# Splitting the gate and value products of a fused feed-forward into three fp32r products

## The reference

```python
def attn_layer(x, Wqkv, qs, ksc, Wo):          # 16 heads of 64, windows of 32, keys of two windows
    q, k, v = jnp.split(x @ Wqkv, 3, -1)
    q, k = rotate(l2norm(q) * qs), rotate(l2norm(k) * ksc)
    return local_attention(q, k, v) @ Wo

def ffn_layer(x, g, bln, W1, b1, W2, b2):
    mu = x.mean(-1, keepdims=True)
    var = ((x - mu) ** 2).mean(-1, keepdims=True)
    xn = (x - mu) / jnp.sqrt(var + 1e-05) * g + bln
    hg = xn @ W1 + b1                           # W1 is 128 x 682
    a, gate = jnp.split(hg, 2, -1)              # 341 columns each
    return a * jax.nn.gelu(gate, approximate=False) @ W2 + b2

for i in range(6):
    x = attn_layer(shift_tokens(x), ...) + x
    x = ffn_layer(shift_tokens(x), ...) + x
```

## Time and profile before

| | us |
|---|---|
| median of 3 runs | 3869.65 (3862.52 to 3872.1) |
| the profiled execution | 3865.56 |
| its span in the profile | 3863.6 |
| layers, first to last projection | about 847 to 3777 |
| one step in the steady part | 61.3 |

### The profile page before, as it was taken

How to read it: one execution, slowest core, us unless ns; L and a number is a source line. 1 busy time by engine, 2 the same in 40 slices (tenths; PEclk the granted TensorE clock), 3 DMA queues, 4 the chain that set the end, 5 groups by cost and what they waited for, 6 DMA issues and landing times. The chain is left out here.

```text
span 3863.6 us, 161420 instructions
## 1 busy us (share of the span) xinstructions
PE 3682.6 (95%) x70608; PEld 2670.3 (69%) x70608; DVE 3257.1 (84%) x4767; ACT 2854.5 (74%) x5060; POOL 2384.6 (62%) x1968
## 2 busy tenths in 40 slices
PE   5899999958999999999999999999999999999997
PEld 3122222237888888888888888888888888888885
DVE  7899999947888888888888888888888888888884
ACT  2588888856777777777777777777777777777774
POOL 2100000047877777787777777777777777777783
PEclk7799999979999999999999999999999999999998
DMA  2110000014344444434444434444444344444442
GB/s 90 34 54 24 22 22 18 10 52 117 103 107 118 105 113 121 108 103 111 120 111 108 117 106 110 117 113 105 110 122 111 104 113 111 123 112 114 108 104 56
DMA packets 202559, 360.11 MB, mean 93 GB/s; under 512 B 35518, under 2 KB 74050, under 8 KB 201538
## 3 DMA queue, kind: packets, MB, share of 16 engines
q1 hardware_dynamic: 201794, 348.71, 33.8%
HBM read 236.68 MB, written 111.67 MB: 90 GB/s over the span
## 5 line engine op out<-in xcount | busy, mean ns | idle before, releaser
L1160 POOL TENSOR_TENSOR T<-T 128x1024 f32<-128x1024 f32 x384 | 908.5, 2378 | 26.7 <-DVE T L1639 25.8
L1178 POOL TENSOR_TENSOR T<-T,rn 128x1024 f32<-128x1024 f32 x384 | 731.1, 1904 | 27.1 <-POOL rn L1171 0.4
L745 ACT ACTIVATE E<-p_s 128x512 f32<-128x512 f32 x1024 | 556.1, 597 | 124.7 <-PE p_s L602 110.6
L1250 PE MATMUL PA<-Wqkv,XS 128*128 128x512 f32 x2304 | 634.2, 411 | 9.5 <-DVE XS L1600 8.7
L678 DVE TENSOR_REDUCE negmax<-p_max 128x1 f32<-128x1024 f32 x512 | 588.8, 1215 | 26.5 <-PE p_max L581 26.4
L1250 PEld LDWEIGHTS PA<-Wqkv,XS 128*128 128x128 f32 x2304 | 415.2, 194 | 80.1 <-DVE XS L1600 10.7
L1647 DVE TENSOR_REDUCE ss<-SQ 128x32 f32<-128x2048 f32 x192 | 436.9, 2275 | 0.0
L1326 PE MATMUL PB<-ET,VW 64*64 64x32 f32 x24576 | 400.7, 220 | 15.9 <-DVE T L1639 9.5
L1326 PEld LDWEIGHTS PB<-ET,VW 64*64 64x64 f32 x24576 | 378.8, 135 | 53.5 <-DVE T L1639 29.7
L1278 PE MATMUL PD<-ident,T 128*128 128x128 f32 x3072 | 409.3, 276 | 6.8 <-POOL T L1178 5.5
L1339 PEld LDWEIGHTS PD<-Wo,OT 128*128 128x128 f32 x3072 | 366.4, 192 | 61.7 <-issue 61.7
(11 more groups left out here) (168 smaller groups left out, 6762.4 us busy)
## 6 DMA issues: line engine op xcount, KB each, us to landing
VW<-v_rows SPq DMA_DIRECT2D x768, 256.0 KB, 4.5
v_rows<-Vs SPq DMA_DIRECT2D x192, 512.0 KB, 5.9
Wraw<-in_Wqkv SPq DMA_DIRECT2D x40, 192.0 KB, 5.2
QA<-parts_q SPq DMA_DIRECT2D x384, 16.0 KB
KA<-parts_k SPq DMA_DIRECT2D x192, 32.0 KB
parts_q<-parts SPq DMA_DIRECT2D x8, 384.0 KB, 2.6
parts_k<-parts SPq DMA_DIRECT2D x8, 384.0 KB, 2.7
Wo<-in_Wo SPq DMA_DIRECT2D x12, 256.0 KB, 4.6
```

Source lines behind the costliest of these rows:

```text
L745: act.activation(E[:, s % 4, c, :], p_s[:, (64 * g + i) % NS, :], ACT.Exp, scale=DH ** -0.5)\
L1160: pool.tensor_tensor(out=t_, in0=t_, in1=T2[:, i * HALF:(i + 1) * HALF], op=ALU.add).then_inc(ad.sem, 1)
L1178: pool.tensor_tensor(out=t_, in0=t_, in1=rn[:, p, i * LH:(i + 1) * LH].unsqueeze(2).broadcast_to([P, LH, LD]), op=ALU.mult).then_inc(no.se ...
L1250: mm = pe.matmul(pair[:, half, :], XS[:, b, i, 1:P + 1], Wqkv[:, l % 2, j, lo:lo + 512], start=(k == 0), stop=(k == 2))
```

## The change

The normalised tokens and `W1` are split into a high part (rounded to fp32r by ACT) and a low part (the rest, by POOL). Each of the six chunk products becomes three fp32r products. `W1` gets zeroed columns behind it, so that each chunk is 128 wide. `fnT` now shares memory with `fx`. Once in each layer ACT and POOL split the weights; once in each step they split the tokens. In PE's code the place of the instructions in the program is set to 98 where it was 100, for two of four slots.

```diff
+    FPAD = FF + NCH * P
+    W1 = m.sb("W1", [P, FPAD])
+    W1s = m.sb("W1s", [P, 2, FPAD], F32R)
+    fnT = fx[:, :, :].rearrange("p b c -> p (b c)")
+    fns = m.sb("fns", [P, 2, B * P], F32R)
 # SP, ahead of load_ff(u // NT)
+                sp.wait_ge(w1s.sem, w1s.at(u // NT - 1))
 # POOL
+        pool.memset(W1[:, 2 * FF:FPAD], 0.0).then_inc(s_one.sem, 1)
+        def ff_split(u):
+            pool.wait_ge(f3e.sem, f3e.at(u))
+            if u > 0:
+                pool.wait_ge(fv.sem, fv.at(u - 1))
+            pool.tensor_tensor(out=fns[:, 1, :], in0=fnT, in1=fns[:, 0, :].bitcast(F32), op=ALU.subtract)\
+                .then_inc(fnl.sem, 1)
+        def split_ff(l):
+            pool.wait_ge(w1s.sem, w1s.at(l, 1))
+            pool.tensor_tensor(out=W1s[:, 1, :], in0=W1[:, :], in1=W1s[:, 0, :].bitcast(F32), op=ALU.subtract)\
+                .then_inc(w1s.sem, 1)
             if is_tile(s - 1):
                 rotate(s - 1, 0)
+            if d == 1 and is_step(u - 2):
+                if (u - 2) % NT == 0:
+                    split_ff((u - 2) // NT)
+                ff_split(u - 2)
             if d == 2 and is_step(u + 1):
                 rotary_table(u + 1)
             if is_tile(s - 1):
                 rotate(s - 1, 1)
 # PE
-    BLOCK, FIRST_Q = 256, (105, 105, 100, 100)
+    BLOCK, FIRST_Q = 256, (105, 105, 98, 98)
+        def ff_product(i, lo):
+            for k, (x, y) in enumerate(((0, 0), (0, 1), (1, 0))):
+                mm = pe.matmul(PC[:, i % 2, :], W1s[:, y, lo:lo + P], fns[:, x, :], start=(k == 0), stop=(k == 2))
+            return mm
         def ff_gate(u, i):
             if i == 0:
                 pe.wait_ge(f3e.sem, f3e.at(u))
+                pe.wait_ge(fnl.sem, fnl.at(u))
+                pe.wait_ge(w1s.sem, w1s.at(u // NT))
-            pe.matmul(PC[0:c, i % 2, :], W1[:, FF + lo:FF + lo + c], fnT[:, :], start=True, stop=True)\
-                .then_inc(fg.sem, 1)
+            ff_product(i, FF + CH[i][0]).then_inc(fg.sem, 1)
         def ff_value(u, i):
-            pe.matmul(PC[0:c, i % 2, :], W1[:, lo:lo + c], fnT[:, :], start=True, stop=True).then_inc(fv.sem, 1)
+            ff_product(i, CH[i][0]).then_inc(fv.sem, 1)
 # ACT
         def ff_norm(u):
             act.wait_ge(s_wf.sem, s_wf.at(u // NT))
+            if u % NT == 0:
+                if u > 0:
+                    act.wait_ge(fv.sem, fv.at(u - 1))
+                act.activation(W1s[:, 0, :], W1[:, :], ACT.Copy).then_inc(w1s.sem, 1)
             act.wait_ge(f3.sem, f3.at(u))
             if u > 0:
+                act.wait_ge(fnl.sem, fnl.at(u - 1))
                 act.wait_ge(fv.sem, fv.at(u - 1))
-            act.activation(fnT[:, :], PC[:, 0, :], ACT.Identity, bias=ln[:, 1:2], scale=ln[:, 0:1])\
+            act.activation(fnT, PC[:, 0, :], ACT.Identity, bias=ln[:, 1:2], scale=ln[:, 0:1])\
                 .then_inc(f3e.sem, 1)
+            act.wait_ge(f3e.sem, f3e.at(u, 1))
+            act.activation(fns[:, 0, :], fnT, ACT.Copy).then_inc(f3e.sem, 1)
 # DVE, ff_tokens
-                dve.wait_ge(f3.sem, f3.at(u - 1))
+                dve.wait_ge(fnl.sem, fnl.at(u - 1))
```

More of the change, by code:

```diff
@@ L929, in layers @@
     KW = 2 * WIN
+    FPAD = FF + NCH * P
     Wraw = m.sb("Wraw", [P, share])
-    W1 = m.sb("W1", [P, 2 * FF])
+    W1 = m.sb("W1", [P, FPAD])
+    W1s = m.sb("W1s", [P, 2, FPAD], F32R)
     W2 = m.sb("W2", [P, NCH, D])
@@ L962, in layers @@
     frs = m.sb("frs", [P, B])
-    fnT = m.sb("fnT", [P, B * P])
+    fnT = fx[:, :, :].rearrange("p b c -> p (b c)")
+    fns = m.sb("fns", [P, 2, B * P], F32R)
     G = m.sb("G", [P, NCH, B * P])
@@ L1022, in layers @@
     f3 = m.count("l_f3")
-    f3e = m.count("l_f3e")
+    f3e = m.count("l_f3e", 2)
+    fnl = m.count("l_fnl")
+    w1s = m.count("l_w1s", 2)
     fg = m.count("l_fg", 3)
@@ L1032, in layers @@
     out = m.count("l_out", 16)
-    READY = 8
+    READY = 9
     def tile(n):
@@ L1056, in load_ff @@
             for dst, src in (
-                (W1[:, :], ins["W1"][l]),
+                (W1[:, 0:2 * FF], ins["W1"][l]),
                 (W2[:, 0:2, :], ins["W2"][l, 0:2 * P].rearrange("(a p) n -> p a n", p=P)),
@@ L1130, in on_pool @@
         pool.memset(zero[:, :], 0.0).then_inc(s_one.sem, 1)
+        pool.memset(W1[:, 2 * FF:FPAD], 0.0).then_inc(s_one.sem, 1)
         pool.memset(three[:, :], 1.5).then_inc(s_one.sem, 1)
-        pool.wait_ge(s_one.sem, 5)
+        pool.wait_ge(s_one.sem, 6)
         pool.memset(HH[lo:lo + 32, NCH - 1, :], 1.0).then_inc(s_one.sem, 1)
@@ L1366, in ff_norm @@
             mm.then_inc(f3.sem, 1)
-            fc_[0] = (f3e.sem, f3e.at(u))
+            fc_[0] = (f3e.sem, f3e.at(u, 1))
+        def ff_product(i, lo):
+            for k, (x, y) in enumerate(((0, 0), (0, 1), (1, 0))):
+                mm = pe.matmul(PC[:, i % 2, :], W1s[:, y, lo:lo + P], fns[:, x, :], start=(k == 0), stop=(k == 2))
+            return mm
         def ff_gate(u, i):
-            lo, c = CH[i]
             if i == 0:
                 pe.wait_ge(f3e.sem, f3e.at(u))
+                pe.wait_ge(fnl.sem, fnl.at(u))
+                pe.wait_ge(w1s.sem, w1s.at(u // NT))
             free(fc_[i % 2])
-            pe.matmul(PC[0:c, i % 2, :], W1[:, FF + lo:FF + lo + c], fnT[:, :], start=True, stop=True)\
-                .then_inc(fg.sem, 1)
+            ff_product(i, FF + CH[i][0]).then_inc(fg.sem, 1)
             fc_[i % 2] = (gd.sem, gd.at(u, i + 1))
         def ff_value(u, i):
-            lo, c = CH[i]
             free(fc_[i % 2])
-            pe.matmul(PC[0:c, i % 2, :], W1[:, lo:lo + c], fnT[:, :], start=True, stop=True).then_inc(fv.sem, 1)
+            ff_product(i, CH[i][0]).then_inc(fv.sem, 1)
             fc_[i % 2] = (hh.sem, hh.at(u, i + 1))
@@ L1697, in ff_down @@
                               op=ALU.add).then_inc(fxd.sem, 1)
-        dve.wait_ge(s_one.sem, 6)
+        dve.wait_ge(s_one.sem, 7)
         for j in range(2):
```

## The result

| | us, median (lowest to highest) | runs |
|---|---|---|
| before | 3870.88 (3862.52 to 3873.27) | 4 |
| after | 4125.57 (4123.97 to 4129.64) | 4 |

The ratio is 1.0664, with a 95% interval of 1.0645 to 1.0682: the change made the kernel 6.6% slower. The profiled execution took 4129.64 us, 264.1 more than the profiled one of before.

What follows compares the result with a forecast made beforehand. PE was taken as the bound, closely followed by POOL. 46 x (5.34 wait + 4.2 clock - 0.36 products) = 422, plus 7 + 1 for the layers, on 3865.56 gave 4295.6, so 4300 us; range 4095 to 4400.

Steps and rivals of the forecast that it cites:

- What bounds the kernel, and POOL's slack: PE is the bound; POOL can be kept about 2.93 us between its rotary additions and normalisations before PE waits.
- POOL's wait: POOL waits 7.0 us between the rotary additions for ACT's high part, moving PE's `attend` in slot 1 by 5.34 us.
- The prices: Durations of ACT's copy (0.63 us), POOL's token and weight subtractions (1.28, 1.8), and two gate chunks on PE (1.47).
- Value products: Three value chunks on PE in slots 2 and 3 save 0.375 us, counted as 0.36 us a step.
- Gate products: Gate chunks on PE in slots 1 and 2 save 0.375 us, given back as a wait for ACT's chain.
- The clock: PE's clock at 0.50 from slot 1's transposes of k in nearly every step, costing 4.2 us a step; bounds 0 to 6.5.
- the forecast's picture: Low clock in slot 1 over transposes of k, `attend` (1.6 us more), the projection of v and the first gate chunks.
- The rows at 885 and 3812: Earlier trace's ends of layers: after `attend` the low clock lasted 3.4 us of full work, around 885 5.6; middle 4.5.
- Code loading: Rival: PE's short stops in slot 1's scores no longer show, or new ones appear elsewhere; 20 us either way, no chance given.
- The clock holds: Rival: same wait on PE, but bursts of transposes keep the clock at 1.00; 4107 us, chance 0.17.
- the forecast's own case: POOL's wait and the clock's fall both cost time on PE's path; 4200 to 4400 us, chance 0.70.

Runs made afterwards that it cites:

- the placement behind both additions: The changed kernel with POOL's two subtractions moved behind the second rotary addition of the same loop; 4019.25 us, ratio 1.0400 against the kernel before.
- the filled gap: The changed kernel with 12 fp32r products put ahead of PE's wait for POOL in slot 1 of each step; 4104.1 us, ratio 1.0618 against the kernel before.

## Why the prediction was right in sign and mechanism, and wrong in size

- **What bounds the kernel, and POOL's slack: right.** 2.93 us of slack, read off and the earlier trace rows, is the point from which the wait counts, and the placement behind both additions confirms it with a second dose (3.13 us measured in its shortest slots, 3.05 by the sum).
- **POOL's wait: right.** Forecast 7.0 us, measured 7.02 in the step shown and 6.94 on the mean. PE's gap ahead of q was to be 3.4 and is 3.47. With the clock held, slot 1 has 19.56 to 19.60 in 34 of 39 steps, 5.5 over the 14.10 of before, where 5.34 was forecast.
- **The prices: right.** Copy 0.63 forecast and 0.632 measured, subtraction 1.28 and 1.290, the one on the weights 1.8 and 1.767. Two gate chunks were to take 1.47 and take 1.40.
- **Value products: right.** 0.36 us a step forecast, slot 3 gained 0.44.
- **Gate products: right.** Their gain was to be given back to ACT's chain; slot 2 went from 15.38 to 15.43, and it became shorter than before only when the gelu was taken away.
- **The clock: wrong, and the whole of the miss.** That it would fall in nearly every round was right: it fell in all 39 steps of the stretch. Its price was put at 4.2 us a step and is 0.47, by the filled gap. (4.2 - 0.47) x 46 = 172 us, and the miss is 174. The step that failed is the one which drew PE's slot 1 as "idle for 3.4 us, 0.9 us of transposes, idle 1.0, 0.9 of transposes, idle 1.0" and let the low level begin to cost from the transposes of k on. Those 0.9 us were taken at the full clock, but the level had fallen already inside the gap of 3.47 us. At the lower level the same eight transposes take 1.86 us, as long as POOL needs for its next piece. So the waits of 1 us that were forecast ahead of the later transposes did not come: PE was fully busy from 1654.76 on, and the level rose again at about 1660, before `attend`. What ran slowly was work that waited for POOL anyway; only the last run of transposes paid, 1660.15 - 1658.48 = 1.67 us against 0.97 in the earlier trace rows. In the next step it paid even less, as PE's rows show:

```profile
1721.84 1.94 PE L1301 MATMUL PD<-ident,T 128*128 128x128 f32 x8 [3.19 <-POOL T L1185]
1723.69 1.56 PE L1332 MATMUL PA<-ident,Ew 128*128 128x128 f32 x8
1725.56 1.06 PE L1301 MATMUL PD<-ident,T 128*128 128x128 f32 x8 [0.30 <-POOL T L1185]
1726.55 2.07 PE L1349 MATMUL PB<-ET,VW 64*64 64x32 f32 x128
```

- **In one step of 39 the forecast's picture came true.** There the level fell only behind the transposes of q, which still ran at the full clock, and lay over `attend` and the projection of v:

```profile
1989.90 1.06 PE L1301 MATMUL PD<-ident,T 128*128 128x128 f32 x8 [3.28 <-POOL T L1185]
...
1995.49 3.64 PE L1349 MATMUL PB<-ET,VW 64*64 64x32 f32 x128
...
1999.19 2.56 PE L1273 MATMUL PA<-Wqkv,XS 128*128 128x512 f32 x6
```

Its slot 2 took 17.69 us where the median is 15.33. `attend` took 1.57 us more than its 2.07, where the forecast had 1.6 more. So the low level cost about what was forecast wherever it lay over this work; what was wrong is when it falls in the other 38 steps. What sets that moment was not looked into.
- The rows at 885 and 3812, from which I had taken the length of the low level, were not at fault. Around 885 it covered 5.6 us of full work, and here about 5, those from the transposes of q on. I had laid that stretch over `attend`, v and the gates instead.
- The Trainium skill (TensorE: Matmul & The Clock Gate, HAM oscillation — how this bites in real kernels) says that such gaps lower the clock once in every round; the windows above agree. What the rule does not say, and I had read into it, is that the low stretch lands on work of the critical path. The page's remark that transposes do not count as work for the gate (Part 4: PE-mode transpose) is not borne out: from 1654.76 until `attend` began at 1660.15 PE ran nothing but transposes, and the window from 1659.6 to 1660.4 has 0.83, so the level was 1.00 for about 0.5 of its 0.8 us and rose at about 1659.9. In the next step the second run of eight (1.56 us where 1.94 is the low level's) is already the faster one.
- **Code loading: no part in it.** The short stops in the scores are still there, 16.2 us in 36 places of the whole execution, where the kernel before has 23.7 in 46; they stand ahead of the longer wait.
- **The number came near a rival for a reason of its own.** "The clock holds" gave 4107; the clock doesn't hold, but its fall is nearly free. That the time lies in the stated range is luck as far as the clock is concerned: the range was drawn down to 4095 to take in that rival, which had a chance of 0.17, while the forecast's own case had 0.70 and 4200 to 4400.

## What to carry to other kernels

An instruction of an in-order engine costs from where it stands: the same subtraction cost about 260 us ahead of a queue that didn't need it, and nothing one slot later. Before a helper is placed, ask when its input is ready, and what is queued behind it at that time. A lower clock is to be priced against the supplier's pace, not by doubling durations: redraw the timeline with the slower durations, and count only what still ends later. Where the fall comes matters as much: a little later, it cost 2.4 us in the same loop. And when a gain does not show, look for the chain that ends within a tenth of a microsecond of the one that was shortened.

## What the runs showed of the hardware that was not expected

- The clamp, a short VectorE instruction whose operands all lie in SBUF, waits in both of its forms for the end of the GpSimd instruction beside it: 0.18 us became 1.36, 1.07, 0.78 and 1.18 us in the rows shown, and each ended within 0.05 us of POOL's. A reduction of 2.27 us at the same place was not lengthened. POOL's load thus reached PE over DVE and ACT, in slots where PE never waits for POOL.
- PE's granted clock fell inside a gap of 3.47 us and rose again during runs of fp32 transposes with nothing else between them. That was so in 29 of the 39 steps; in the other ten `attend` took 2.12 to 3.64 us and not 2.07, so the low level reached into it.
- A subtraction on POOL whose two inputs are the same tile took 1.04 us for 128x512, and one with two different inputs 1.29. The type of the result is no part of it, as a product of the same size in plain fp32 took 1.28. Why was not looked into.
